# First utterance of an audio tower: the late parts of queries and keys of four heads go from SBUF to SBUF, and ScalarE's queue issues the other eight loads

## The chip, the core and the metric

The kernel runs on one core of one Trainium2 chip. A core has five engines that run their own instruction streams and meet only at semaphores: TensorE (PE, with its weight loads PEld), VectorE (DVE), ScalarE (ACT), GpSimd (POOL) and SyncE (SP), which only issues transfers here. All transfers run on the core's 16 DMA engines. The metric is the device time of one execution in microseconds (us).

## The reference

The input is 16 utterances of 750 frames with 23 features. A time-delay layer (five neighbouring frames, 115 taps, to 128 channels, ReLU, batch normalisation over all frames) gives h. Then come an attention layer and a mixture-of-experts layer, each on the layer norm of h and added to it:

```python
h = relu(patches @ W.T + b); h = batchnorm(h)            # 16 x 746 x 128
q, k, v = heads(layernorm(h) @ Wq.T + bq), ...           # 8 heads of 16
scores = einsum('bhqd,bhkd->bhqk', q, k) / sqrt(16)
h = h + merge(softmax(scores) @ v) @ Wo.T + bo
e = argmax(xf @ Wr + br)                                 # top 1 of 8 experts, xf = layernorm(h)
h = h + gate * (relu(xf @ W1[e] + b1[e]) @ W2[e] + b2[e])   # gate: softmax over one logit, 1
```

## The kernel before, in words

**Stages.** First the time-delay layer of all utterances is computed and kept in `seq`. Then a software pipeline of bodies i = -2 ... 16 follows, each of 72 steps. In body i the scores and probabilities of utterance i are computed, the row maxima of utterance i+1 from step 24 on (and those of utterance i in steps 0 to 23), and layer norm, queries, keys and values of utterance i+2 are prepared. Body -2 (FIRST_BODY) holds only the preparation of utterance 0; body -1 holds the preparation of utterance 1 and, from step 24, the first 48 steps of maxima of utterance 0. At the end tiles of tokens sorted by expert go through their expert's two layers.

**Queries and keys in parts.** A score must be as exact as in float32 but is computed in bf16: each of q and k is split into three bf16 parts (part 0 the rounded value, parts 1 and 2 what is left), made in `q_part` and `k_part` with channels on the 128 partitions. The matmul wants, for each head, 96 partitions: six groups of 16 (n = 0 ... 5), each a part of the head's 16 channels: `Q_PARTS = (0, 0, 1, 1, 0, 2)`, `K_PARTS = (0, 1, 0, 1, 2, 0)`. As heads lie on partitions in `q_part` and beside each other in `q_rows` (in `arena`) and `k_rows`, every part is stored to DRAM (`store_q`, `store_k`: q_parts_dram, k_parts_dram) and loaded from there (`load_parts`, line 506), one transfer for each of the six groups n, for q and for k, for the first four heads (group g = 0) and for the last four (g = 1): 24 loads an utterance. PE's maxima of utterance b start when 12 loads of g = 0 have landed (`pe.wait_ge(s_ld[0], b * 192 + 192)`); those of g = 1 are needed 36 steps later.

**Order of SP in the first two bodies.** Body -2: `store_q` of parts 0, 1, 2, each when its part is there; `store_k(0)`; `load_first_heads`: wait for all three query stores, six query loads, `store_k(1)`, `store_k(2)`, then for each part a wait for that store and its key loads. Body -1 begins with the twelve loads of g = 1. In body -2 `split` runs on DVE (lines 420 to 424), in the others on POOL.

**What else lies there.** At the start of body -1, ACT, DVE and PE compute a few constants (`constants`, lines 1383 to 1390 on PE, 835 to 838 on ACT, 1034 and 1036 on DVE): PE works on a product, ACT copies it out (`wo_t`, line 835), PE goes on with it, and so on, until DVE writes `row_c` (line 1036). POOL waits for that (`s_cv`), then adds to h_cur and writes `seq` (line 710); only then ACT may overwrite `h_cur` with utterance 1 (line 798, two halves at steps 8 and 11, PE's transposes of line 1319 before each). DVE takes its statistics (line 968), POOL merges them, takes the root (line 702) and normalises into xn (line 411, six tiles). At steps 35 and 39 PE transposes xn (line 1319). Each engine works strictly through its own stream, so PE's transpose at step 35 also holds up the maxima that stand behind it; DVE's statistics stand ahead of its first maxima (lines 1192 and 1195: two reductions of 512 columns and one of 468 for three steps). Three PSUM banks lie between PE's score products for the maxima and DVE's reductions.

Of the kernel before, what the change touches and what calls it, by code (L numbers as in the profile page):

```python
# [5 lines left out]
def audio_tower(  # L6
# [33 lines left out]
    L = T - CONTEXT + 1  # L40
    HALF = L // 2
    H = 8
    DH = D // H
# [3 lines left out]
    GH = 4  # L47
# [17 lines left out]

    Q_PARTS = (0, 0, 1, 1, 0, 2)
    K_PARTS = (0, 1, 0, 1, 2, 0)
    KR = len(Q_PARTS) * DH
    KM = KR + 2

# [4 lines left out]
    STEPS = 2 * HALF_STEPS  # L75
# [28 lines left out]
    with ctx:  # L104
# [3 lines left out]
        def sem(name):  # L108
            return ctx.enter_context(nc.semaphore(name))
# [150 lines left out]
        s_q_w = sem("s_q_w")  # L260
        s_k_w = [sem(f"s_k_w{n}") for n in range(3)]
        s_ld = [sem(f"s_ld{g}") for g in range(2)]
        s_mrow = sem("s_mrow")
        s_turn = sem("s_turn")
        s_rt = sem("s_rt")
# [44 lines left out]
        def live(i, ahead):  # L310

            return not isinstance(i, int) or 0 <= i + ahead < B
# [92 lines left out]
        def is_body(i, number):  # L405
            return isinstance(i, int) and i == number
# [56 lines left out]
        def load_patches(engine, c, low, high):  # L463
# [3 lines left out]
            engine.dma_start(patches[CONTEXT * low:CONTEXT * high, t0:t1], taps)\  # L467
                  .then_inc((s_frames if low == 0 else s_rest)[c], 16)

        def load_tok_w(engine, low, high):  # L470
            engine.dma_start(tok_w_sb[CONTEXT * low:CONTEXT * high, :],
                             tok_w.rearrange("(k f) d -> f k d", f=FEAT)[low:high, :, :]).then_inc(s_tokw, 16)
# [6 lines left out]
        def _(sp):  # L479
# [17 lines left out]
            sp.dma_start(rows_dram[DEAD:DEAD + D, :], pad_row[:, :]).then_inc(s_pad, 16)  # L497

            def load_parts(par, g, name, wanted, i, steps):
                dst, src, parts = {"Q": (q_rows, q_dram, Q_PARTS), "K": (k_rows, k_dram, K_PARTS)}[name]  # L500
                for n, part in enumerate(parts):
                    if part in wanted:
                        step = next(steps)
                        if 0 <= i + step // STEPS < B:
                            sp.wait_ge(s_st, scores(i, step))
                        sp.dma_start(dst[par][DH * n:DH * (n + 1), GH * g:GH * (g + 1), 0:L],
                                     src[64 * g:64 * (g + 1), part, :].rearrange("(h j) t -> j h t", j=DH))\
                          .then_inc(s_ld[g], 16)

            def store_q(i, parts):  # L510
                for part in parts:
                    if part == 0:
                        sp.wait_ge(s_free, fill(i, "Q", 1))
                    else:
                        sp.wait_ge(s_split, (i + 2) * 6 + part + 1)
                    sp.dma_start(q_dram[:, part, :], q_part[:, part, :]).then_inc(s_q_w, 16)

            def store_k(i, part):
                if part == 0:
                    sp.wait_ge(s_free, fill(i, "K", 1))  # L520
                else:
                    sp.wait_ge(s_split, (i + 2) * 6 + part + 4)
                sp.dma_start(k_dram[:, part, :], k_part[:, part, :]).then_inc(s_k_w[part], 16)

            def load_first_heads(i, par):
                sp.wait_ge(s_q_w, (i + 2) * 48 + 48)
                steps = iter(LOAD0_AT)
                load_parts(par, 0, "Q", (0, 1, 2), i, steps)
                for part in range(3):
                    if is_body(i, FIRST_BODY) and part > 0:  # L530
                        store_k(i, part)
                for part in range(3):
                    sp.wait_ge(s_k_w[part], (i + 2) * 16 + 16)
                    load_parts(par, 0, "K", (part,), i, steps)

            def body(i, par):
                if live(i, 1):
                    wait(sp, s_st, i * STEPS if live(i, -1) else 0)
                    load_parts(1 - par, 1, "Q", (0, 1, 2), i, iter(LOAD1_AT))
                if live(i, 0):  # L540
                    sp.wait_ge(s_free, fill(i, "MAX1", 0))
                    for n in range(2):
                        sp.dma_start(q_rows[par][KR + n:KR + n + 1, GH:H, :],
                                     max_rows[1][QUAD * n:QUAD * n + GH * NT, :]).then_inc(s_mrow, 16)
                if live(i, 1):
                    load_parts(1 - par, 1, "K", (0, 1, 2), i, iter(LOAD1_AT[6:]))
                if live(i, 2):
                    wait(sp, s_ld[1], (i + 2) * 192)
                    store_q(i, range(3 if is_body(i, FIRST_BODY) else 1))
                    store_k(i, 0)  # L550
                if live(i, 1):
                    sp.wait_ge(s_free, fill(i, "MAX0", 0))
                    for n in range(2):
                        sp.dma_start(q_rows[1 - par][KR + n:KR + n + 1, 0:GH, :],
                                     max_rows[0][QUAD * n:QUAD * n + GH * NT, :]).then_inc(s_mrow, 16)
                if isinstance(i, int) and i == W_LAST + 1:
                    sp.wait_ge(s_ln2, W_LAST + 1)
                    sp.dma_start(w_sb[:, :, W1:W1 + HID], w1.rearrange("e p n -> p e n")).then_inc(s_w, 16)
                    for e in range(E):
                        sp.dma_start(w_sb[:, e, W2:W2 + HID].rearrange("p (j n) -> p j n", j=JH),  # L560
                                     w2[e].rearrange("(j p) n -> p j n", p=128)).then_inc(s_w, 16)
                    sp.dma_start(w_sb[:, :, B2:B2 + D], b2.partition_broadcast(128)).then_inc(s_w, 16)
                    sp.dma_start(w_sb[:, :, B1:B1 + JH], b1).then_inc(s_w, 16)
                if live(i, 2):
                    if not is_body(i, FIRST_BODY):
                        store_q(i, (1, 2))
                        store_k(i, 1)
                        store_k(i, 2)
                    if live(i, 0):
                        sp.wait_ge(s_st, scores(i, HALF_STEPS - 1))  # L570
                    load_first_heads(i, par)
# [199 lines left out]
        def _(act):  # L771
# [35 lines left out]
            def q_or_k(i, name, half, k):  # L807

                full, part, bias, scale = {"Q": (q_full, q_part, bq4, SCALE), "K": (k_full, k_part, bk_sb, 1.0)}[name]
                dst = (full[:, :] if k == 0 else part[:, 0, :])[:, HALF * half:HALF * (half + 1)]  # L810
                if k == 0:
                    act.wait_ge(s_misc, fill(i, name, half))
                    in_turn(act, i, name, half)
                    if name == "Q":
                        wait(act, s_q_w, (i + 2) * 48)
                    else:
                        for n in range(3):
                            wait(act, s_k_w[n], (i + 2) * 16)
                last = nc.scalar.activation(dst, bank(i, name, half)[:, 0:HALF], ACT.Identity, bias=bias[:, 0:1], scale=scale)
                if k == 1:  # L820
                    last.then_inc(s_free, 1)
# [41 lines left out]
            def body(i, par):  # L863
# [4 lines left out]
                for s in range(STEPS):  # L868
# [39 lines left out]
                        nc.scalar.activation(g_exp[:, :], g_diff[:, :], ACT.Exp).then_inc(s_gate, 1)  # L908
                    if s in H_AT and live(i, 3):
                        normed(i + 3, H_AT.index(s))  # L910
                    if is_body(i, LAST_BODY) and s in ACT_SLOTS:
                        n = ACT_SLOTS[s]
                        if n < 0:
                            xt_evac(0, 0)
                        else:
                            act_turn(n, n % ROUND, n // ROUND)
# [371 lines left out]
        def _(pe):  # L1288
# [140 lines left out]
            def body(i, par):  # L1429
# [6 lines left out]
                for s in range(STEPS):  # L1436
# [15 lines left out]
                    if 0 <= b < B:  # L1452

                        u, t, n = m // (3 * NT), m % (3 * NT) // 3, m % 3
                        if m % HALF_STEPS == 0:
                            pe.wait_ge(s_ld[m // HALF_STEPS], b * 192 + 192)
                        wait(pe, s_red, b * STEPS + (m + 1 - N_MX))
                        if n < 2:
                            quad(mx_bank[m % N_MX][:, 0:WIDE_Q], q_rows[b % 2][0:KR, 2 * u + n, D * t:D * (t + 1)],
                                 k_rows[b % 2][0:KR, 2 * u + n, 0:WIDE_Q]).then_inc(s_mx, 1)  # L1460
                        else:
                            for a in range(2):
                                last = quad(mx_bank[m % N_MX][:, NARROW_Q * a:NARROW_Q * (a + 1)],
                                            q_rows[b % 2][0:KR, 2 * u + a, D * t:D * (t + 1)],
                                            k_rows[b % 2][0:KR, 2 * u + a, WIDE_Q:L])
                            last.then_inc(s_mx, 1)
# [65 lines left out]
```

## Time and profile before

| what | us |
|---|---|
| median of 3 runs | 1179.86 (1179.08 to 1182.18) |
| the profiled execution's own time | 1180.77 |
| its span from first to last instruction | 1178.9 |
| PE, DVE, ACT, POOL busy | 1119.5, 1042.9, 912.1, 686.8 |
| first product for maxima of utterance 0 | at 69.28 |

Times in the rows are microseconds from the span's start. PEclk is the granted clock of TensorE: 1.00 is 2.4 GHz and 0.50 is 1.2 GHz. SPq and ACTq are the issuing of transfers by these engines: how long the sequencer was taken up by the issue, not when the data landed. A queue's row such as "x6" is that many issues in a row.

### The profile page before, as it was taken

The page shows a single profiled execution, that of the slowest core. Times are in us where ns is not written, and L with a number is a line of the kernel's source. Part 1 is how long each engine was busy: PE and PEld are TensorE (multiplying, and loading weights), DVE is VectorE, ACT ScalarE, POOL GpSimd, SP SyncE. Part 2 cuts the span into 40 slices and gives each one's busy share as a digit, 9 for nine tenths or more (in the row PEclk, how much of TensorE's full clock was granted, in tenths as well). Part 3 has the DMA queues.
Part 4 walks back from the last instruction along what each step waited for, and adds up shares of the span by engine and source line. Part 5 has one row for each costly group of instructions (what it writes and reads, how often), then busy time and mean ns, then how long its engine had stood idle before and what let it go on. Part 6 is the DMA issues. An engine that isn't in the chain of part 4 may idle for free.

```text
span 1178.9 us, 51282 instructions
## 1 busy us (share of the span) xinstructions
PE 1119.5 (95%) x20483; PEld 728.7 (62%) x20483; DVE 1042.9 (88%) x2404; ACT 912.1 (77%) x2125; POOL 686.8 (58%) x926
## 2 busy tenths in 40 slices
PE   6479999999999999999999999999999999999996
PEld 3323556565656565655656565656565558899996
DVE  8569899999999999999999999999999947777774
ACT  5425888888988888888888888888887885577774
POOL 2052618575766667585858576666653256666664
PEclk9769999999999999999999999999999999999998
DMA  8052121423233231313141323223231623434331
GB/s 199 33 98 83 46 82 43 115 66 96 75 82 94 62 98 52 105 52 107 43 115 61 99 75 84 86 69 97 55 105 38 191 60 92 118 115 117 110 100 47
DMA packets 81192, 102.21 MB, mean 87 GB/s; under 512 B 17964, under 2 KB 74787, under 8 KB 80526
## 3 DMA queue, kind: packets, MB, share of 16 engines
q1 hardware_dynamic: 72416, 79.03, 25.3%
q0 software_dynamic: 8384, 20.22, 5.1%
q8 instruction: 152, 2.49, 0.9%
q14 instruction: 54, 0.44, 0.1%
q10 hardware_dynamic: 186, 0.02, 0.0%
HBM read 60.76 MB, written 38.93 MB: 85 GB/s over the span
## 4 chain that ended last, share of the span: by engine, by line
PE 52%; DVE 36%; DMA 3%; issue 2%; ACT 2%; SPq 1%; DVEq 0%; POOL 0%; POOLq 0%; ACTq 0%
PE psum L1314 27%; DVE half_max L1192 18%; PE psum L1376 9%; DVE half_max L1195 8%; PE psum L1405 7%; PE psum L1417 7%; DVE stats L968 2%; DMA arena<-max_rows 1%; PE psum L1319 1%; DVE by_tok L1008 1%; DVE rows L1049 1%; DVE merged_t L1029 1%; ACT arena L875 1%; PE psum L1396 1%; DVE pos_i L1104 1%
## 5 line engine op out<-in xcount | busy, mean ns | idle before, releaser
L1192 DVE TENSOR_REDUCE half_max<-psum 128x1 f32<-128x512 f32 x768 | 511.4, 677 | 28.9 <-PE psum L1314 28.0
L875 ACT ACTIVATE arena<-psum 128x512 f32<-128x512 f32 (+1 forms) x768 | 423.2, 604 | 61.2 <-PE psum L1314 55.7
L1314 PE MATMUL psum<-k_rows,arena 96*32 96x512 bf16 (+1 forms) x6144 | 462.1, 326 | 8.1 <-DMA k_rows<-k_parts_dram 5.0
L1314 PE MATMUL psum<-arena,k_rows 98*32 98x512 bf16 (+1 forms) x6144 | 457.6, 322 | 4.0 <-DMA arena<-max_rows 2.2
L1376 PE MATMUL psum<-arena,values 128*32 128x234 f32 (+3 forms) x3072 | 313.4, 477 | 1.2 <-ACT arena L878 0.8
L1314 PEld LDWEIGHTS psum<-k_rows,arena 96*32 96x32 bf16 x6144 | 176.8, 97 | 139.8 <-DVE half_max L1192 27.6
L1314 PEld LDWEIGHTS psum<-arena,k_rows 98*32 98x32 bf16 x6144 | 176.9, 96 | 132.1 <-issue 42.1
L1195 DVE TENSOR_REDUCE half_max<-psum 128x2 f32<-128x468 f32 x384 | 242.3, 631 | 2.5 <-PE psum L1314 2.4
L878 ACT ACTIVATE arena<-psum 128x468 f32<-128x468 f32 (+1 forms) x384 | 197.9, 571 | 28.0 <-PE psum L1314 25.4
L665 POOL DMA_INDIRECT routed_rows_dram<-rows,pos_i x96 | 97.0, 1011 | 91.5 <-PE psum L1314 61.5
L646 POOL DMA_INDIRECT out_dram<-k_rest,slot_id x85 | 101.8, 1197 | 61.4 <-DVE k_rest L1170 46.0
L1376 PEld LDWEIGHTS psum<-arena,values 128*32 128x32 f32 (+1 forms) x3072 | 97.9, 110 | 35.2 <-issue 1.8
L676 POOL TENSOR_TENSOR m_diff<-stats 128x6 f32<-128x6 f32 x15 | 3.0, 201 | 141.6 <-DVE stats L968 141.6
L856 ACT COPY xn_t<-psum 128x128 f32<-128x128 f32 x101 | 26.8, 265 | 66.4 <-PE psum L1396 64.8
L1405 PE MATMUL psum<-xn_t,values 128*128 128x128 f32 x536 | 72.2, 278 | 1.3 <-DVE values L1154 1.3
L411 POOL TENSOR_SCALAR arena<-h_cur,m_mean,rstd 128x128 f32<-128x128 f32 x90 | 70.5, 793 | 3.3 <-POOL rstd L702 3.2
L411 POOL TENSOR_SCALAR rows<-rows,n_mean,rstd 128x128 f32<-128x128 f32 x90 | 71.8, 806 | 0.0
L1405 PEld LDWEIGHTS psum<-xn_t,values 128*128 128x128 f32 x536 | 65.9, 194 | 2.6 <-DVE values L1154 1.7
L1154 DVE COPY values<-seq 128x1156 f32 x67 | 53.1, 792 | 9.5
L420 POOL TENSOR_TENSOR q_rest<-q_full,q_part 128x746 f32<-128x746 f32 x15 | 24.2, 1615 | 54.2 <-DVE onehot L1079 37.5
L1008 DVE STREAM_TRANSPOSE by_tok<-o_un 128x384 f32<-128x384 f32 x64 | 36.3, 567 | 12.5 <-ACT o_un L888 12.5
L1405 PE MATMUL psum<-xn_t,seq 128*128 128x128 f32 x272 | 36.7, 278 | 4.2 <-DVE seq L1154 3.7
(237 smaller groups left out, 1603.3 us busy)
## 6 DMA issues: line engine op xcount, KB each, us to landing
arena<-q_parts_dram SPq DMA_DIRECT2D x192, 93.2 KB, 2.6
k_rows<-k_parts_dram SPq DMA_DIRECT2D x192, 93.2 KB, 2.5
q_parts_dram<-q_part SPq DMA_DIRECT2D x48, 186.5 KB
k_parts_dram<-k_part SPq DMA_DIRECT2D x48, 186.5 KB, 1.9
q_full<-routed_rows_dram SPq DMA_DIRECT2D x34, 130.0 KB
k_full<-routed_rows_dram SPq DMA_DIRECT2D x34, 130.0 KB
q_rest<-routed_rows_dram SPq DMA_DIRECT2D x33, 130.0 KB
arena<-in_x_t_dram SPq DMA_DIRECT2D x3, 703.1 KB, 17.0
```

What stands on the lines that cost most here:

```text
L411: last = ops.tensor_scalar(dst(t), src(t), mean_var[:, t, 0:1], r_root[:, t:t + 1], ALU.subtract, ALU.mult)
L646: pool.indirect_dma_start(out=out_rows, out_offset=bass.IndirectOffsetOnAxis(ap=slot_id[:, n:n + 1], axis=0), in_=slot_y[n][:, :], in_offs ...
L665: pool.indirect_dma_start(out=rows_dram, out_offset=bass.IndirectOffsetOnAxis(ap=pos_i[:, t:t + 1], axis=0), in_=rows[:, t, :], in_offset= ...
L875: nc.scalar.activation(probs[0:kn(kt), kt % N_P, j, :], st_bank[s % N_ST][0:kn(kt), 0:WIDE_Q], ACT.Exp).then_inc(s_exp, 1)
L878: nc.scalar.activation(narrow_probs[0:kn(kt), kt, NARROW_Q * j:NARROW_Q * (j + 2)], st_bank[s % N_ST][0:kn(kt), 0:2 * NARROW_Q], ACT.Exp). ...
L1154: nc.vector.tensor_copy(slot_w[n % N_W].unsqueeze(1), w_sb[:, bass.ds(e, 1), :]).then_inc(s_fw, 1)
L1192: nc.vector.tensor_reduce(half_max[:, n, part:part + 1], mx_bank[m % N_MX][:, 0:WIDE_Q], AX.X, ALU.max)\
L1195: nc.vector.tensor_reduce(half_max[:, n, 2:4], mx_bank[m % N_MX][:, 0:2 * NARROW_Q].rearrange("p (a t) -> p a t", a=2), AX.X, ALU.max).the ...
L1314: last = nc.tensor.matmul(dst[n:n + m], weights[:, n:n + m], moving, start=start, stop=stop)
L1376: last = nc.tensor.matmul(o_bank[32 * j:32 * (j + 1), 0:WIDE_Q if wide else NARROW_Q], values[b % 3][0:kn(kt), kt, GH * g + j, :], moving, ...
L1405: last = nc.tensor.matmul(psum[:, 2 + n % 2, D * k:D * (k + 1)], slot_w[n % N_W][:, W1 + D * k:W1 + D * (k + 1)], slot_xt[n % 2][:, :], st ...
L1417: last = nc.tensor.matmul(psum[:, 5 + n % 2, 0:D], slot_ht[n % 2][:, D * k:D * (k + 1)], slot_w[n % N_W][:, W2 + D * k:W2 + D * (k + 1)], ...
```

## The change

In body -2 SP stores part 0 and 1 of q and part 0 of k as before. For g = 0 the groups that hold part 2 of q (one), part 1 of k (two) and part 2 of k (one) no longer come from DRAM: SP copies them from `q_part` and `k_part` straight into `q_rows` and `k_rows`, one transfer for each group and head, 16 in all, each of 16 partitions. After them SP stores the three late parts (they are still loaded from DRAM for g = 1) and waits for all stores. The other eight loads of g = 0 are issued by ACT at the end of body -2, ahead of its share in `constants`: five for q after two q stores have landed, three for k after the store of part 0. PE waits for both groups of transfers. In every other body SP does what it did; ACT and PE get one wait more, in body -1, on a semaphore of the copies.

```diff
+    DIRECT = (("Q", 2), ("K", 1), ("K", 2))
+    N_DIRECT = Q_PARTS.count(2) + K_PARTS.count(1) + K_PARTS.count(2)
...
+        def load_rows(engine, par, g, name, n):
+            dst, src, parts = {"Q": (q_rows, q_dram, Q_PARTS), "K": (k_rows, k_dram, K_PARTS)}[name]
+            engine.dma_start(dst[par][DH * n:DH * (n + 1), GH * g:GH * (g + 1), 0:L],
+                             src[64 * g:64 * (g + 1), parts[n], :].rearrange("(h j) t -> j h t", j=DH))\
+                  .then_inc(s_ld[g], 16)
...
+            def direct(i, par, name, part):
+
+                dst, src, parts, k = {"Q": (q_rows, q_part, Q_PARTS, 1), "K": (k_rows, k_part, K_PARTS, 4)}[name]
+                sp.wait_ge(s_split, (i + 2) * 6 + part + k)
+                for n in range(len(parts)):
+                    if parts[n] == part:
+                        for h in range(GH):
+                            sp.dma_start(dst[par][DH * n:DH * (n + 1), h, 0:L], src[DH * h:DH * (h + 1), part, :])\
+                              .then_inc(s_direct, 16)
+
+            def first_heads(i, par):
+
+                store_q(i, (0, 1))
+                store_k(i, 0)
+                for name, part in DIRECT:
+                    direct(i, par, name, part)
+                sp.wait_ge(s_q_w, 32)
+                store_q(i, (2,))
+                store_k(i, 1)
+                store_k(i, 2)
+                sp.wait_ge(s_q_w, 48)
+                for part in range(3):
+                    sp.wait_ge(s_k_w[part], 16)
...
             def body(i, par):
+                if is_body(i, FIRST_BODY):
+                    first_heads(i, par)
+                    return
...
                     if name == "Q":
                         wait(act, s_q_w, (i + 2) * 48)
+                        if is_body(i, FIRST_BODY + 1):
+                            act.wait_ge(s_direct, GH * N_DIRECT * 16)
...
+                    if is_body(i, FIRST_BODY) and s == STEPS - 1:
+                        act.wait_ge(s_q_w, 32)
+                        for n in (0, 1, 4, 2, 3):
+                            load_rows(act, par, 0, "Q", n)
+                        act.wait_ge(s_k_w[0], 16)
+                        for n in (0, 2, 5):
+                            load_rows(act, par, 0, "K", n)
...
                         if m % HALF_STEPS == 0:
-                            pe.wait_ge(s_ld[m // HALF_STEPS], b * 192 + 192)
+                            if b == 0 and m == 0:
+                                pe.wait_ge(s_direct, GH * N_DIRECT * 16)
+                            pe.wait_ge(s_ld[m // HALF_STEPS], b * 192 + 192 - (0 if m else 16 * N_DIRECT))
```

## Rows read from the trace of the kernel before

**Rows 1.** The page's chain that ended last, by engine

```profile
PE 52%; DVE 36%; DMA 3%; issue 2%; ACT 2%; SPq 1%; DVEq 0%; POOL 0%; POOLq 0%; ACTq 0%
```

**Rows 2.** The chain, 30 to 110 us: start, us, what

```profile
55.76 2.52 DMA q_parts_dram<-q_part
...
65.60 3.64 DMA k_rows<-k_parts_dram
...
69.28 3.15 PE psum L1314 x30
...
79.55 2.38 PE psum L1314 x25
```

**Rows 3.** Timeline of SP's queue: start, us, line, transfer, issues

```profile
53.12 2.96 SPq L516 DMA_DIRECT2D q_parts_dram<-q_part  x3
56.13 0.43 SPq L523 DMA_DIRECT2D k_parts_dram<-k_part  x1
58.30 2.68 SPq L506 DMA_DIRECT2D arena<-q_parts_dram  x6
...
66.06 2.77 SPq L506 DMA_DIRECT2D arena<-q_parts_dram  x6
```

**Rows 4.** Waits, 40 to 75 us: total, times, longest

```profile
PE psum L1314 <- DMA k_rows<-k_parts_dram: 5.0, 1, 5.0
```

**Rows 5.** Timeline of ACT, 56 to 77 us; idle before in brackets

```profile
56.51 0.48 ACT L829 COPY values<-psum 128x384 f32<-128x384 f32 x1
57.64 0.27 ACT L835 COPY o_un<-psum 128x128 f32<-128x128 f32 x1 [0.65 <-PE psum L1384]
...
62.82 0.48 ACT L798 COPY h_cur<-psum 128x384 f32<-128x384 f32 x1 [2.98 <-POOL seq L710]
64.35 0.48 ACT L798 COPY h_cur<-psum 128x384 f32<-128x384 f32 x1 [1.05 <-PE psum L1319]
```

**Rows 6.** Timeline of PE in the same stretch

```profile
58.60 0.57 PE L1387 MATMUL psum<-wv_sb,o_un 128*128 128x8 f32 x2 [0.99 <-DVE bo_all L1034]
...
63.36 0.90 PE L1319 MATMUL psum<-ident,h_t 128*128 128x128 f32 x3 [2.13 <-ACT h_cur L798]
...
75.85 0.90 PE L1319 MATMUL psum<-ident,arena 128*128 128x128 f32 x3
```

**Rows 7.** Timeline of DVE, 53 to 70 us

```profile
57.32 0.94 DVE L424 TENSOR_TENSOR k_part<-k_rest,k_part 128x746 bf16<-128x746 f32 x1
...
64.86 1.26 DVE L968 BATCH_NORM_STATS2 stats<-h_cur 128x6 f32<-128x128 f32 x6 [4.17 <-ACT h_cur L798]
...
69.95 1.29 DVE L1192 TENSOR_REDUCE half_max<-psum 128x1 f32<-128x512 f32 x2 [3.83 <-PE psum L1314]
```

**Rows 8.** Timeline of POOL, 60 to 76 us

```profile
60.99 1.80 POOL L710 TENSOR_TENSOR seq<-h_cur,bo_all 128x768 f32<-128x768 f32 x1
66.20 0.20 POOL L676 TENSOR_TENSOR m_diff<-stats 128x6 f32<-128x6 f32 x1 [3.41 <-DVE stats L968]
...
69.65 4.69 POOL L411 TENSOR_SCALAR arena<-h_cur,m_mean,rstd 128x128 f32<-128x128 f32 x6 [0.22 <-POOL rstd L702]
```

**Rows 9.** ACT's own queue at the kernel's start, its only issues

```profile
0.80 0.40 ACTq L773 DMA_DIRECT2D tok_b_sb<-in_tok_b_dram  x1
1.23 1.39 ACTq L471 DMA_DIRECT2D by_tok<-in_tok_w_dram  x1
```

**Rows 10.** Stretches: PE, PEld, DVE, ACT, POOL busy, PEclk, DMA share, GB/s

```profile
58.00:60.00 2.00, 0.98 (x4) 0.72 (x4) 0.45 (x2) 0.33 (x2) 0.00 (x0) 0.50 0.31 70
...
66.00:68.00 2.00, 0.00 (x0) 0.00 (x0) 0.12 (x1) 0.01 (x1) 1.49 (x8) 0.50 1.05 154
...
80.00:82.00 2.00, 2.00 (x40) 1.10 (x36) 1.28 (x3) 0.30 (x2) 0.00 (x0) 0.62 0.00 0
...
94.00:96.00 2.00, 1.40 (x22) 0.59 (x26) 2.00 (x6) 0.51 (x2) 1.92 (x2) 0.79 0.00 0
```

**Rows 11.** Small transfers issued by SP at the start (0.1 KB)

```profile
30.80 0.61 SPq L493 DMA_DIRECT2D bv_sb<-in_bv_dram  x1
```

More of the change, by code:

```diff
@@ L262, in audio_tower @@
         s_ld = [sem(f"s_ld{g}") for g in range(2)]
+        s_direct = sem("s_direct")
         s_mrow = sem("s_mrow")
@@ L499, in load_parts @@
             def load_parts(par, g, name, wanted, i, steps):
-                dst, src, parts = {"Q": (q_rows, q_dram, Q_PARTS), "K": (k_rows, k_dram, K_PARTS)}[name]
-                for n, part in enumerate(parts):
+                for n, part in enumerate({"Q": Q_PARTS, "K": K_PARTS}[name]):
                     if part in wanted:
@@ L505, in load_parts @@
                             sp.wait_ge(s_st, scores(i, step))
-                        sp.dma_start(dst[par][DH * n:DH * (n + 1), GH * g:GH * (g + 1), 0:L],
-                                     src[64 * g:64 * (g + 1), part, :].rearrange("(h j) t -> j h t", j=DH))\
-                          .then_inc(s_ld[g], 16)
+                        load_rows(sp, par, g, name, n)
+            def direct(i, par, name, part):
[18 more added lines that the diff above has]
+                    sp.wait_ge(s_k_w[part], 16)
             def store_q(i, parts):
@@ L529, in load_first_heads @@
                 for part in range(3):
-                    if is_body(i, FIRST_BODY) and part > 0:
-                        store_k(i, part)
-                for part in range(3):
                     sp.wait_ge(s_k_w[part], (i + 2) * 16 + 16)
@@ L548, in body @@
                     wait(sp, s_ld[1], (i + 2) * 192)
-                    store_q(i, range(3 if is_body(i, FIRST_BODY) else 1))
+                    store_q(i, (0,))
                     store_k(i, 0)
@@ L564, in body @@
                 if live(i, 2):
[L565 to L568, printed above, removed]
+                    store_q(i, (1, 2))
+                    store_k(i, 1)
+                    store_k(i, 2)
                     if live(i, 0):
```

## The prediction

> **What bounds the kernel now.** I read the page's chain first: nine tenths of it are PE and DVE [rows 1], so transfers matter only where both stand still. The chain of the stretch in question, ahead of the first maxima, is different: store of q part 2 (2.52 us), loads and key stores behind it, the last key load (3.64), and then PE at 69.28 [rows 2]. The waits say what that costs: PE idles 5.0 us before its first product for maxima, on a key load [rows 4]. PE had finished its last earlier work at 63.36 + 0.90 = 64.26 [rows 6]. So the loads are late by 5.0 us, and that is what the change can attack.
>
> Next I read what stands behind. PE transposes xn at 75.85, in its place among the maxima (step 35) [rows 6]. POOL finishes xn at 69.65 + 4.69 = 74.34 [rows 8]. So if the maxima started earlier, PE would get to step 35 earlier, but xn would be there only at 74.34: of the 5.0 us only 75.85 - 74.34 = 1.5 us can be won as long as POOL's chain stays where it is. The bound after the change is therefore not the loads but the chain that makes xn. Back from POOL's 69.65: merge from 66.20 [rows 8], DVE's statistics from 64.86 [rows 7], ACT's two copies into h_cur at 62.82 and 64.35, the first waiting for POOL's line 710 [rows 5], which starts at 60.99 [rows 8] after DVE's last constant, and that chain of constants passes through ACT's copy of wo_t at 57.64 [rows 5]. Nothing in it has slack: from 58.60 on each row starts as the one before ends.
>
> **The change part by part.**
>
> *ACT's eight issues.* They stand in ACT's stream between the values copy, which ends at 56.51 + 0.48 = 56.99, and the copy of wo_t at 57.64 [rows 5]. First ACT waits for two q stores. The third store went out at 55.76 and took 2.52 us [rows 2]; the second goes out one DVE subtraction (0.94, [rows 7] shows its twin) earlier, at 54.8, so it lands near 57.3. An issue costs SP (2.68 + 0.04) / 6 = 0.45 us, and (2.77 + 0.05) / 6 = 0.47 when the DMA engines are full [rows 3]. ACT's own two issues took 0.40 and 1.39 us [rows 9]: these are the two ends. I take 0.46, since the transfers are those that SP issued, unchanged in shape, and ACT's first issue (0.40) is near to it. The k store of part 0, now issued ahead of the third q store's place, at 56.13 at the latest [rows 3], lands before the sixth load's turn. ACT is done at 57.3 + 8 x 0.46 = 61.0.
>
> *What waits behind them.* The copy of wo_t starts at 61.0 instead of 57.64, 3.4 late. PE's line 1387 had waited until 58.60 for DVE as well [rows 6]; now it starts 0.05 after wo_t's 0.27, at 61.3: 2.7 us late. All that follows is a chain without slack and moves by 2.7: POOL's line 710 to 63.7, ACT's h_cur copies to 65.5 and 67.1, PE's second transpose of h_t to 66.1, done at 67.0, DVE's statistics to 67.6, done at 68.85, POOL's normalisation to 72.35, done at 77.05.
>
> *The loads.* Eight by ACT from 57.3 on (746 KB), sixteen copies by SP (16 x 23.9 KB = 382 KB): the same bytes as twelve loads before. The DMA engines were used to 0.31 from 58 to 60 and to 1.05 from 66 to 68, where they moved 154 GB/s [rows 10]; at that pace 1.13 MB need 7.3 us, and part of it starts at 55.8: landed by about 64.5 to 65.5. ACT's last load is issued at 60.5 and takes at most the 3.64 of the last key load [rows 2]: 64.2.
>
> *SP's sixteen copies.* Four follow the q split (about 55.8), eight and four the k splits, whose last ends at 58.26 [rows 7]. The issues bound them, not the splits: 55.8 + 16 x 0.46 = 63.2, and the last one, issued at 62.8, lands between 2.52 and 3.64 later [rows 2]: 65.3 to 66.4. No row shows a copy from SBUF to SBUF. Ends for an issue: 0.40, the smallest that ACT's queue shows [rows 9], and 0.61 with 0.04 between two, the small ones of SP at the start [rows 11]; the latter puts the last issue at 65.6 and its landing at 69.2. The far end is the 1.39 [rows 9], rival D. I take 0.46, as a store and loads of unlike shape cost SP nearly the same, 0.43 and 0.45 [rows 3]. The three late stores then go out at about 63.3 to 64.7 and land near 68, so the twelve loads of the other four heads begin at about 68 instead of 66.06 and end at 73.6; they are needed 36 steps after the first product, near 88. That is hidden, and would cost something only beyond 14 us.
>
> *First maxima.* PE is free at 67.0, the data are there at 66.4. So PE starts at about 67.0 instead of 69.28. DVE's statistics, which stand ahead of its first reduction, end at 68.85, so DVE starts at 68.9 instead of 69.95: 1.05 us of lead. At DVE's pace, the same as before, PE would be at step 35 at 75.85 - 1.05 = 74.8. There xn is missing until 77.05. PE starts that transpose at 77.1 instead of 75.85, idle 2.3 us and DVE with it, and everything behind it is 77.1 - 75.85 = 1.25 us late. The 5.0 us wait on loads is thus gone, and a wait on POOL stands in its place.
>
> *From there to the end.* From 75.9 to the end the chain is PE and DVE with small parts of others, so I let 1.25 us go through undiminished. The additional waits on landed copies are passed long before. The sum: 1180.77 + 1.25 = 1182.0 against the profiled execution. Against the median of the runs, which is 0.9 lower, it is 1181.1, and this is my number.
>
> *The clock.* The granted clock is 0.50 from 58 on and rises near 81 (0.62 in 80 to 82), when the query products begin, and is 0.79 in 94 to 96 [rows 10]. Until 81.94 the chain is on PE [rows 2], so a rise that comes later or earlier relative to the work counts. The wait of 2.3 us lies in a stretch that is at 1.2 GHz anyway. I put nothing for it and keep 1 us to each side.
>
> *Rules of the Trainium skill.* The trace shows full DMA engines (1.05) only from 60 on [rows 10] and SP issuing one load every 0.46 us. "DMA: Bandwidth & Descriptors", section "Issuing engines are not separate DMA queues", says that issuing from several engines saves only the sequencer's time for the issue, as all run on the same 16 DMA engines. By that rule the transfers gain only what lay in SP's sequence; it agrees with the bound by bytes above. The same page, "Rules for kernel authors", says that transfers under 64 KB pay mostly overhead; it speaks against sixteen copies of 23.9 KB, and by it they would be the last to land, as they are in my working too; their landing at 69.2 by the dearer issue would still leave the sum as it is.
>
> **The rivals.**
>
> *A, forecast: ACT's issues push the constants.* 1181.1, as worked out. For it: the stream order and the absence of slack.
>
> *B: ACT's issuing is cheap or does not hold up its copies.* Then POOL's chain stays, xn is there at 74.34, the maxima start with the data at about 66, PE waits at step 35 until 74.35: 1.5 us won, 1178.4. Against it: ACT's queue shows 0.40 and 1.39, nothing near zero [rows 9].
>
> *C, the other side: ACT's issues are dear.* If an issue on ACT's queue beside a busy SP costs the 1.39 [rows 9], eight cost 11.1 us, ACT is free at 68.4, wo_t's successor is 10.1 late, xn at 84.4, and the loss is 84.45 - 75.85 = 8.6: 1188.5. It becomes slower by more than 3.5 us from about 0.74 us for an issue on. Against it: the 1.39 is one transfer of another shape, at a time when the whole input was being loaded.
>
> *D: the copies come late.* Before, step 35 came 75.85 - 69.28 = 6.57 after the first product. Landed at 69.2 they bring it at 75.8, still before xn's 77.05, and the result is A's. They decide only if they land after 77.05 - 6.57 = 70.5, that is from 0.74 us an issue on; at 0.9 they are there at 55.8 + 15 x 0.9 + 3.64 = 72.9, step 35 comes at 79.5, 3.7 late: 1183.6. Nothing but the 1.39 speaks for it.
>
> **How the numbers follow.** About 0.3%, 3.5 us, is what a measurement can tell from no change. A 0.66, B 0.15, C 0.12, D 0.07. A and B lie within 0.3% wholly, up to noise of runs (the three shown span 3.1 us); of C three quarters are over it, of D half; noise and the clock put a little on both sides. Slower 0.14, same 0.82, faster 0.04. The range takes in B's 1178.4 and D's 1183.6 with something for noise: 1178.2 to 1184.3; what is left out is mostly C.
>
> **What would show it.** In the profile after: eight ACTq issues of 0.43 to 0.47 us between 57 and 61; the copy of wo_t at about 61; PE's first product for maxima near 67 and DVE's first reduction near 68.9; PE's wait at step 35 on POOL's line 411, about 2.3 us, ending near 77.1; scores of utterance 0 starting at 100.4 instead of 99.2. A is wrong if wo_t is copied before 60 (B), after 63 (C), if the first product waits on a transfer until after 70 (D), or if the time leaves 1178 to 1184.

## The result and the profile after

| | before | after |
|---|---|---|
| median of 12 runs, us | 1180.13 (1177.32 to 1182.18) | 1182.86 (1180.96 to 1185.69) |
| ratio, 95% interval | | 1.0023 [1.0014, 1.0032] |
| the profiled execution and its span, us | 1180.77, 1178.9 | 1184.05, 1182.0 |
| first product for maxima | 69.28 | 67.81 |
| PE's transpose of xn, step 35 | 75.85 | 78.14 |

The change costs 2.7 us, 0.23%: real by its interval, and less than the 0.3% that I had set as the bound of a change. It is also more than the 1.25 that I had forecast: 1.25 us are a ratio of 1.0011, just below the interval. Of the eleven executions of e1_sp_issues below, one took 4211.93 us and is left out of its ratio. The first maxima do start 1.5 us earlier; the time is lost behind them. The wait on loads [rows 4] is gone and another has taken its place. Waits of the kernel after, 40 to 78 us (total, times, longest):

```profile
PE psum L1352 <- DVE half_max L1230: 1.1, 1, 1.1
...
PEld psum L1352 <- DMA k_rows<-k_part: 0.3, 1, 0.3
```

and, in the same view up to 85 us, the one that counts:

```profile
PE psum L1357 <- POOL arena L414: 2.5, 1, 2.5
```

The timeline of ACT after shows where it comes from. In [rows 5] the copy of wo_t (L835 there, L866 here; the profile calls the tile o_un, whose memory wo_t uses) began 0.65 us behind the end of the values copy; now eight issues stand between:

```profile
56.81 0.48 ACT L860 COPY values<-psum 128x384 f32<-128x384 f32 x1
57.03 2.90 ACTq L475 DMA_DIRECT2D arena<-q_parts_dram  x5
59.97 1.86 ACTq L475 DMA_DIRECT2D k_rows<-k_parts_dram  x3
61.87 0.27 ACT L866 COPY o_un<-psum 128x128 f32<-128x128 f32 x1 [4.57 <-issue]
...
66.44 0.48 ACT L827 COPY h_cur<-psum 128x384 f32<-128x384 f32 x1 [2.99 <-POOL seq L739]
```

SP's queue after. The sixteen copies (L523) take 0.62 to 0.63 us each (2.48 / 4, 7.54 / 12), and the late stores follow only then:

```profile
56.08 2.48 SPq L523 DMA_DIRECT2D arena<-q_part  x4
58.60 7.54 SPq L523 DMA_DIRECT2D k_rows<-k_part  x12
66.25 0.50 SPq L546 DMA_DIRECT2D q_parts_dram<-q_part  x1
66.80 0.91 SPq L553 DMA_DIRECT2D k_parts_dram<-k_part  x2
71.59 2.67 SPq L475 DMA_DIRECT2D arena<-q_parts_dram  x6
```

PE, DVE and POOL after, to be laid beside [rows 6 to 8]. PE's products start, stop for DVE's statistics, go on, and then PE stands before step 35 until POOL's row is over (73.28 + 4.72 = 78.00; xn lies in `arena`, so the rows call it that):

```profile
66.98 0.90 PE L1357 MATMUL psum<-ident,h_t 128*128 128x128 f32 x3 [2.13 <-ACT h_cur L827]
67.81 1.44 PE L1352 MATMUL psum<-k_rows,arena 96*32 96x512 bf16 x16
70.39 5.23 PE L1352 MATMUL psum<-k_rows,arena 96*32 96x512 bf16 x48 [1.14 <-DVE half_max L1230]
78.14 0.87 PE L1357 MATMUL psum<-ident,arena 128*128 128x128 f32 x3 [2.53 <-POOL arena L414]
```

```profile
68.48 1.26 DVE L1006 BATCH_NORM_STATS2 stats<-h_cur 128x6 f32<-128x128 f32 x6 [4.17 <-ACT h_cur L827]
69.66 1.27 DVE L1230 TENSOR_REDUCE half_max<-psum 128x1 f32<-128x512 f32 x2
```

```profile
64.61 1.80 POOL L739 TENSOR_TENSOR seq<-h_cur,bo_all 128x768 f32<-128x768 f32 x1
...
73.28 4.72 POOL L414 TENSOR_SCALAR arena<-h_cur,m_mean,rstd 128x128 f32<-128x128 f32 x6 [0.21 <-POOL rstd L731]
```

The chain of the kernel after has no transfer in this stretch any more; it goes through POOL:

```profile
73.28 0.81 POOL arena L414
...
74.10 3.91 POOL arena L414 x5
78.01 0.14 issue
78.14 0.87 PE psum L1357 x3
```

The delay lasts. In the chains of the two kernels the long row of score products of utterance 0 begins at 99.19 before and at 101.41 after, 2.22 later, where step 35 was 2.29 later:

```profile
99.19 5.63 PE psum L1314 x92
```

```profile
101.41 5.63 PE psum L1352 x92
```

### The profile page after: what moved, and what is told of

The parts are those of the page before. It is cut to its first block, busy times and chain, and to the rows that moved or that the text cites. A ratio compares the mean times of both kernels' runs of the same rounds, so it can differ in the third digit from the quotient of the medians.

```text
span 1182.0 us, 51298 instructions
## 1 busy us (share of the span) xinstructions
PE 1121.0 (95%) x20483; PEld 730.0 (62%) x20483; DVE 1043.7 (88%) x2404; ACT 913.0 (77%) x2125; POOL 690.0 (58%) x926
## 4 chain that ended last, share of the span: by engine, by line
PE 50%; DVE 37%; issue 3%; DMA 2%; ACT 2%; POOL 1%; SPq 0%; DVEq 0%; POOLq 0%; ACTq 0%
PE psum L1352 25%; DVE half_max L1230 19%; PE psum L1414 9%; DVE half_max L1233 8%; PE psum L1443 7%; PE psum L1455 6%; DVE stats L1006 2%; DMA arena<-max_rows 1%; PE psum L1357 1%; DVE by_tok L1046 1%; DVE rows L1087 1%; DVE merged_t L1067 1%; ACT arena L906 1%; PE psum L1434 1%; DVE pos_i L1142 1%
```

## The experiments

The end of the values copy, from which everything here is counted, lies at 56.99 in the profile of before and at 55.9 to 58.3 in the others: executions differ by that much before they come to the changed part: the second store of q stands as much earlier or later in each. So the table gives distances from that end, one profiled execution each, and the time from all runs. "Start" is the first product for maxima, "step 35" PE's transpose of xn, "against before" the difference of step 35 to the first row. "At the scores" is the same difference for ACT's first exponential of utterance 0, some 24 us behind step 35.

| kernel | wo_t | xn ready | start | step 35 | against before | at the scores | ratio to before |
|---|---|---|---|---|---|---|---|
| before | 0.65 | 17.35 | 12.29 | 18.86 | | | 1 |
| after | 4.58 | 20.71 | 10.52 | 20.85 | +1.99 | +1.92 | 1.0023 [1.0014, 1.0032] |
| e1_sp_issues | 0.65 | 17.38 | 14.01 | 20.58 | +1.72 | +2.92 | 1.0012 [1.0000, 1.0024] |
| e4_before_idle | 3.25 | 19.34 | 13.32 | 19.89 | +1.03 | +1.09 | 1.0004 [0.9994, 1.0015] |
| e5_no_copies | 3.65 | 19.77 | 9.88 | 19.92 | +1.06 | +1.21 | 1.0013 [1.0004, 1.0022] |
| e3_gaps | 0.65 | 16.78 | 10.16 | 16.92 | -1.94 | -1.82 | 0.9988 [0.9977, 1.0000] |
| e3_gaps_again | 0.64 | 17.23 | 10.18 | 17.37 | -1.49 | -0.32 | 0.9990 [0.9978, 1.0002] |
| e7_gaps_no_copies | 0.65 | 17.37 | 10.17 | 17.51 | -1.35 | -0.53 | 0.9978 [0.9967, 0.9989] |
| e2_after_constants | 0.64 | 18.04 | 11.72 | 18.29 | -0.57 | +0.62 | 0.9990 [0.9977, 1.0003] |
| e6_after_idle | 9.63 | 25.75 | 15.58 | 25.89 | +7.03 | +7.09 | 1.0059 [1.0041, 1.0077] |

In every row step 35 comes at the later of two: 0.14 or 0.15 behind xn, or 6.57 behind the start. The start decides in the kernel before, in e1_sp_issues, in e4_before_idle and in e2_after_constants, xn in the others. The theory is that the time follows the column of step 35; the rivals were the copies, the transfers' traffic and the start itself. Times 1180 us, each ratio's interval holds its row's difference at step 35 (for the change 1.7 to 3.8, for e7_gaps_no_copies -3.9 to -1.3).

The column of the scores is less tidy. In e1_sp_issues, e2_after_constants, e3_gaps_again and e7_gaps_no_copies 0.8 to 1.2 us are lost between step 35 and the scores. In these four executions the granted clock rises later: PEclk is 0.62 in 80 to 82 before [rows 10] and 1.00 in 82 to 84, and in the last three it is 0.50 and then 0.81 to 0.89, though step 35 stands 1.0 to 1.6 us earlier in the span than before; in e1_sp_issues it is 0.50 until 86, with step 35 only 2.7 us later. e7_gaps_no_copies, columns as in [rows 10]:

```profile
80.00:82.00 2.00, 2.00 (x32) 0.76 (x28) 1.18 (x3) 1.03 (x2) 0.00 (x0) 0.50 0.04 8
```

No experiment moves the clock alone, so it is likely but not shown that the late rise costs this microsecond, and nothing shows how many other executions have it. The intervals of e1_sp_issues, e2_after_constants and e7_gaps_no_copies leave out what their one profiled execution has at the scores: one profile stands for the order of events, and only the runs for the time.

**e1_sp_issues: ACT issues nothing.** The edit, on the kernel after:

```diff
-                for name, part in DIRECT:
-                    direct(i, par, name, part)
+                direct(i, par, "Q", 2)
+                sp.wait_ge(s_q_w, 32)
+                for n in (0, 1, 4, 2, 3):
+                    load_rows(sp, par, 0, "Q", n)
+                sp.wait_ge(s_k_w[0], 16)
+                for n in (0, 2, 5):
+                    load_rows(sp, par, 0, "K", n)
+                direct(i, par, "K", 1)
+                direct(i, par, "K", 2)
...
-                    if is_body(i, FIRST_BODY) and s == STEPS - 1:
-                        act.wait_ge(s_q_w, 32)
-                        for n in (0, 1, 4, 2, 3):
-                            load_rows(act, par, 0, "Q", n)
...
```

> The change with the eight loads issued by SP itself, between the copies of q part 2 and those of k; ACT issues nothing. Theory (ACT's eight issues hold up its copy of wo_t and with it xn): wo_t is copied near 57.7 again, POOL starts line 739 near 61.0 and ends xn near 74.4; SP issues 24 transfers from 55.8 on, which at 0.46 us each end at 66.8 and land near 69.5, so the first product comes at 69.5 and step 35 at 76.0: time as before, 1180.1 (ratio to before 1.000). If a copy from SBUF costs SP 0.62 us by its kind, as in the profile of the change, and not because ACT issues beside it, the sixteen copies show 0.62 here too, SP ends at 69.5, the first product comes at 72 and the time is 2.5 us above before. Rival (the copies themselves or the order of stores cost the 2.7 us): 2.7 above before with wo_t early.

Its SP queue and PE timeline:

```profile
56.70 2.47 SPq L523 DMA_DIRECT2D arena<-q_part  x4
59.22 2.45 SPq L475 DMA_DIRECT2D arena<-q_parts_dram  x5
61.72 1.36 SPq L475 DMA_DIRECT2D k_rows<-k_parts_dram  x3
63.12 7.47 SPq L523 DMA_DIRECT2D k_rows<-k_part  x12
```

```profile
71.94 6.64 PE L1352 MATMUL psum<-k_rows,arena 96*32 96x512 bf16 x64 [6.74 <-DMA k_rows<-k_part]
```

xn is back at its old distance (17.38), and the start is 1.7 late, because a copy from SBUF costs SP 0.62 us with no other queue at work, where a load in the same queue costs 0.49 or 0.45 (2.45 / 5, 1.36 / 3). So 0.62 is the price of this kind of copy: the second reading of the expectation, though 2.5 us was too much for it. With ACT silent the copies leave the chain of xn as it was; what they cost is the late start. The time (1.0000 to 1.0024) separates this run clearly neither from before nor from the change, so here the profile speaks and not the time.

**e4_before_idle: eight useless issues on ACT in the kernel before.** Nothing waits for them but ACT itself, in the last body.

```diff
...
+                    if is_body(i, FIRST_BODY) and s == STEPS - 1:
+                        for n in range(8):
+                            act.dma_start(idle_in[:, n, :, :], x_t[0:16, 0:4, 8 * n:8 * (n + 1)]).then_inc(s_idle, 16)
...
```

> The kernel before with eight more transfers, issued by ACT at the end of body -2, that nobody needs: 16 partitions by 4 pieces of 32 bytes each, 2 KB, so the engines carry nothing to speak of. All loads stay with SP. Theory: the eight issues alone push wo_t to 60.7 (0.46 each, if the 0.60 seen in the change came from two queues issuing at once) or 61.8 (0.60 each, if it is ACT's own price); xn ends 2.7 to 3.7 later than 74.34; the maxima still start at 69.3 with the loads; PE transposes xn at 77.1 to 78.1 instead of 75.85; time 1.2 to 2.3 above before, 1181.4 to 1182.4. Rival (the late xn is harmless, the loss of the change came from its transfers): time as before, 1180.1.

```profile
56.37 0.35 ACTq L916 DMA_DIRECT2D idle_in<-in_x_t_dram  x1
...
56.75 3.34 ACTq L916 DMA_DIRECT2D idle_in<-in_x_t_dram  x7
60.13 0.27 ACT L837 COPY o_un<-psum 128x128 f32<-128x128 f32 x1 [3.24 <-issue]
```

```profile
58.06 2.67 SPq L508 DMA_DIRECT2D arena<-q_parts_dram  x6
```

ACT pays 0.48 an issue (3.34 / 7) and xn is 2.0 later, not the 2.7 or more of the expectation. The useless issues wait for no store, so they began at 56.37, half a microsecond before the values copy ended, and wo_t is only 2.60 late (3.25 - 0.65). Of that PE had waited 0.64 for DVE anyway: its next product began at 58.60 [rows 6], and could have begun 0.05 behind wo_t's end, at 57.64 + 0.27 + 0.05 = 57.96. Then 1.4 of slack at step 35 (18.86 - 17.35 - 0.14) swallow most of the 2.0, and what moves step 35 by 1.0 is the start, itself 1.0 late: SP's six key loads took 4.55 instead of 4.06, and from their end to the start 3.93 passed instead of 3.26. Why is open. The time cannot be told from before. This run shows that ACT's issues delay xn, and that alone, with the slack still there, it costs next to nothing; it does not show what a late xn costs. It shows one thing more: ACT's last four issues run beside SP's six loads without a pause (58.06 to 60.73), and neither queue is slower for it: 0.48 on ACT, and 2.67 for SP's six where they took 2.68 before [rows 3].

**e5_no_copies: ACT issues as in the change, the late groups come from DRAM.**

```diff
...
-                for name, part in DIRECT:
-                    direct(i, par, name, part)
                 sp.wait_ge(s_q_w, 32)
                 store_q(i, (2,))
                 store_k(i, 1)
                 store_k(i, 2)
                 sp.wait_ge(s_q_w, 48)
-                for part in range(3):
-                    sp.wait_ge(s_k_w[part], 16)
+                load_rows(sp, par, 0, "Q", 5)
+                sp.wait_ge(s_k_w[1], 16)
+                load_rows(sp, par, 0, "K", 1)
+                load_rows(sp, par, 0, "K", 3)
+                sp.wait_ge(s_k_w[2], 16)
+                load_rows(sp, par, 0, "K", 4)
+                sp.wait_ge(s_k_w[0], 16)
...
```

> The change without the copies on chip: ACT issues the same eight loads at the same place, SP stores all three parts of q and k and then loads the four late groups from DRAM, as before the change. Theory: the ACT chain is as in the change, so wo_t at 60.8 to 61.9, xn at 77.1 to 78.0, time as the change, 1.2 to 2.5 above before. It tells what an ACT issue costs when SP issues hardly anything beside it (five stores and loads in place of sixteen copies): 0.46 if the price came from two queues at once, 0.60 if it is ACT's own. First product near 67. Rival (the copies cost the time): as before, 1180.1.

Its ACT queue and PE timeline:

```profile
56.94 2.30 ACTq L472 DMA_DIRECT2D arena<-q_parts_dram  x5
59.28 1.50 ACTq L472 DMA_DIRECT2D k_rows<-k_parts_dram  x3
60.83 0.27 ACT L854 COPY o_un<-psum 128x128 f32<-128x128 f32 x1 [3.64 <-DMA q_parts_dram<-q_part]
```

```profile
67.06 1.44 PE L1340 MATMUL psum<-k_rows,arena 96*32 96x512 bf16 x16 [0.23 <-DMA k_rows<-k_parts_dram]
...
77.10 0.87 PE L1345 MATMUL psum<-ident,arena 128*128 128x128 f32 x3 [2.53 <-POOL arena L411]
```

The same shapes issued at the same place cost ACT 0.46 to 0.50 here and 0.58 to 0.62 in the change: without SP's sixteen copies beside them they have the price that I had predicted, and step 35 is 1.06 late, near my 1.25. The loads from DRAM are there at 9.88. That is no proof that they are faster than the copies: in the change PE was busy until it started at 10.52, and the trace has the last copy landed at 67.44, distance 10.15. Where PE waits for nothing but the transfers, the two are level, 10.16 with copies (e3_gaps) and 10.17 without (e7_gaps_no_copies). The copies are not needed for the early start, and with them ACT's issues are dearer. That is read from the profiles: the intervals of the times, 1.0004 to 1.0022 here and 1.0014 to 1.0032 in the change, overlap.

**e3_gaps: the eight issues in ACT's idle time.** One ahead of the copy of wo_t, two behind it, five behind the last constant; the copies stay.

```diff
...
                 nc.scalar.copy(wo_t, st_bank[0][:, 0:D]).then_inc(s_ca, 1)
+                for n in (1, 4):
+                    load_rows(act, 0, 0, "Q", n)
...
                 if is_body(i, FIRST_BODY + 1):
                     constants()
+                    for n in (2, 3):
+                        load_rows(act, 1 - par, 0, "Q", n)
+                    act.wait_ge(s_k_w[0], 16)
+                    for n in (0, 2, 5):
+                        load_rows(act, 1 - par, 0, "K", n)
...
                         act.wait_ge(s_q_w, 32)
-                        for n in (0, 1, 4, 2, 3):
-                            load_rows(act, par, 0, "Q", n)
-                        act.wait_ge(s_k_w[0], 16)
-                        for n in (0, 2, 5):
-                            load_rows(act, par, 0, "K", n)
+                        load_rows(act, par, 0, "Q", 0)
```

> The change with ACT's eight issues spread over the idle time in its share of the constants: one ahead of the copy of wo_t (0.65 us idle there), two behind it (1.6 us idle), five after the last constant (3.0 us idle); copies by SP as in the change. Theory: no copy of ACT is delayed by more than 0.3 us, POOL starts line 739 near 61.0, xn ends near 74.4; the loads are issued by 62.9 and land near 66, SP's copies near 67.5, the first product comes near 67.5 and step 35 near 74.4: 1.5 us below before, 1178.7, and 4.2 below the change. Rival (transfers or the clock hold up the start whoever issues): first product near 69, time as before or above.

```profile
58.09 0.36 PE L1428 MATMUL psum<-wv_sb,o_un 128*128 128x8 f32 x2 [0.94 <-DVE bo_all L1075]
...
66.70 6.64 PE L1355 MATMUL psum<-k_rows,arena 96*32 96x512 bf16 x64 [3.51 <-DMA k_rows<-k_part]
73.46 0.87 PE L1360 MATMUL psum<-ident,arena 128*128 128x128 f32 x3
```

The same transfers from the same queues as in the change, only elsewhere in ACT's stream: step 35 is 3.9 us earlier than in the change, and the time 0.9988 and, once more as e3_gaps_again, 0.9990, where step 35 is 3.5 earlier. Neither interval alone excludes before; both exclude the change's 1.0023. Half a microsecond of this profile is not the edit's: PE's constant took 0.36 here and 0.57 in [rows 6], at a PEclk of 0.82 in 58 to 60 instead of 0.50 [rows 10], and xn came 0.57 earlier than before. e3_gaps_again has xn within 0.12 of before.

> The kernel of e3_gaps once more, to narrow its interval beside e7_gaps_no_copies: 1.4 to 2 us below before, ratio 0.9983 to 0.9988.

**e7_gaps_no_copies: e3_gaps with the edit of e5_no_copies.**

> ACT's eight issues spread over its idle time as in e3_gaps, but no copies on chip: SP stores the late parts and loads the four late groups from DRAM as in e5_no_copies. In e5_no_copies the last of those loads let PE start at 67.06, about as early as the copies did in e3_gaps (66.70, with the values copy there 0.6 earlier). Theory (the gain of e3_gaps is that the eight loads leave SP's queue without holding up ACT, and xn then bounds; the copies do nothing for it): PE transposes xn within 0.3 us of where it does in e3_gaps, counted from the end of the values copy (16.9 us behind it; 18.9 in the kernel before), time 1.4 below before, 1178.6. Rival (the copies are what makes the early start possible): first product as in the kernel before, time 1180.

Its ACT, PE and POOL timelines:

```profile
56.87 0.48 ACT L848 COPY values<-psum 128x384 f32<-128x384 f32 x1
57.19 0.35 ACTq L472 DMA_DIRECT2D arena<-q_parts_dram  x1
58.00 0.27 ACT L854 COPY o_un<-psum 128x128 f32<-128x128 f32 x1 [0.65 <-PE psum L1413]
58.01 0.83 ACTq L472 DMA_DIRECT2D arena<-q_parts_dram  x2
...
60.76 1.39 ACTq L472 DMA_DIRECT2D k_rows<-k_parts_dram  x3
63.19 0.48 ACT L817 COPY h_cur<-psum 128x384 f32<-128x384 f32 x1 [2.98 <-POOL seq L729]
```

```profile
67.52 6.64 PE L1343 MATMUL psum<-k_rows,arena 96*32 96x512 bf16 x64 [2.89 <-DMA k_rows<-k_parts_dram]
74.86 0.88 PE L1348 MATMUL psum<-ident,arena 128*128 128x128 f32 x3 [0.70 <-POOL arena L411]
```

```profile
70.02 4.70 POOL L411 TENSOR_SCALAR arena<-h_cur,m_mean,rstd 128x128 f32<-128x128 f32 x6 [0.22 <-POOL rstd L721]
```

Step 35 follows xn by 0.14, with half of the change left out. Its distance of 17.51 is within the expected 0.3 of e3_gaps_again's 17.37, not of e3_gaps's 16.92, which had the faster constants. The time is 1178.07, ratio 0.9978 [0.9967, 0.9989]: it beats the kernel before by 2.3 us by the medians, more than the 1.4 that was expected, and the change by about 5 us (0.9978 against 1.0023). Whether it is better than e3_gaps the intervals do not tell.

**e2_after_constants: all eight issues behind the last constant.**

```diff
                 if is_body(i, FIRST_BODY + 1):
                     constants()
+                    act.wait_ge(s_q_w, 32)
+                    for n in (0, 1, 4, 2, 3):
+                        load_rows(act, 1 - par, 0, "Q", n)
+                    act.wait_ge(s_k_w[0], 16)
+                    for n in (0, 2, 5):
+                        load_rows(act, 1 - par, 0, "K", n)
...
```

> The change with all eight of ACT's issues in one place behind its last constant, where it is idle for 3.0 us before it copies h_cur. Theory: 8 x 0.60 = 4.8 us there (SP issues copies beside it) delay the h_cur copy by 1.8 us, or by 0.7 at 0.46 each; xn ends 0.7 to 1.8 later than in the kernel before, less the 1.5 of slack at step 35: between 0.8 below and 0.3 above before, 1179.3 to 1180.4, which is 2.3 to 3.4 below the change. Rival (any issue on ACT costs the same wherever it stands): as the change, 1182.9.

```profile
58.10 0.34 ACTq L475 DMA_DIRECT2D arena<-q_parts_dram  x1
...
58.47 1.98 ACTq L475 DMA_DIRECT2D arena<-q_parts_dram  x4
60.49 1.85 ACTq L475 DMA_DIRECT2D k_rows<-k_parts_dram  x3
62.45 0.48 ACT L827 COPY h_cur<-psum 128x384 f32<-128x384 f32 x1 [4.02 <-issue]
```

The h_cur copy waits for the end of the issues, about 1.1 us, and xn is 0.7 late; step 35 comes 0.57 earlier than before. It is not xn that sets it here but the start, at 11.72 (11.72 + 6.57 = 18.29): the copies, issued as early as in e3_gaps, landed 1.5 us later than there. The expectation had not seen that, and why they did is open. By the profile it is a dearer place than the gaps and a cheaper one than ahead of the constants; the times exclude the change (the interval ends at 1.0003) but do not tell this place from the gaps. The price of an issue depends on what it stands in front of.

**e6_after_idle: the eight useless issues, in the change, behind its own eight.**

> The change with eight more transfers of 2 KB on ACT, behind its eight loads and ahead of its copy of wo_t, that nobody needs (64 pieces of 32 bytes each). Theory (each issue on ACT ahead of the constants is paid in full once xn is the bound): 8 x 0.46 to 0.60 = 3.7 to 4.8 us on top of the change, PE's transpose of xn that much later, first product 3.7 to 4.8 later too, as PE's transposes of h_t wait in the same chain: 1186.5 to 1187.6. Rival (something behind hides it, or the loss of the change came from elsewhere): 1183.

```profile
62.89 5.03 ACTq L953 DMA_DIRECT2D idle_in<-in_x_t_dram  x8
67.96 0.27 ACT L868 COPY o_un<-psum 128x128 f32<-128x128 f32 x1 [9.63 <-issue]
```

Eight issues of 2 KB each cost 5.03 us, move xn by 25.75 - 20.71 = 5.04 and the time from 1.0023 to 1.0059, 4.2 us (six runs; the two intervals together allow about 2 to 6.5); the profiled step 35 is 7.03 behind that of before and the time 0.0059 x 1180 = 7.0. Against e4_before_idle, where nearly the same issues cost nothing that the time shows, this is the whole point: the slack at step 35, about 1.4 us, is spent once, and from then on every issue is paid in full, at 0.63 here beside SP's copies and 0.48 there.

## Why the prediction was right, point by point

- **The bound.** Right, and nearly in size: the 1.5 us that the loads' 5.0 could give are 1.4, as PE starts the transpose 0.14 behind xn. e3_gaps_again and e7_gaps_no_copies got 1.5 and 1.35 at step 35, e3_gaps 1.9 with an xn that was 0.57 early by itself, the change nothing.
- **ACT's issues hold up the constants, and no slack follows.** Right, and shown: wo_t is 3.93 late by the table, POOL's line 739 3.32 and xn 3.36, which is 3.93 less the 0.64 that PE had waited for DVE anyway, as the prediction had subtracted (3.4 to 2.7). Taking the issues out of the way (e3_gaps, e7_gaps_no_copies) gives it back; doubling them (e6_after_idle) adds their full duration.
- **The price of an issue on ACT.** The mis-sized term: 0.46 taken, 2.94 / 5 = 0.59 and 0.62 measured with the gaps between, so 4.8 us for eight instead of 3.7: 1.1 us. e5_no_copies shows that 0.46 to 0.50 is right without the copies beside.
- **The copies.** 0.62 instead of 0.46, near the upper row that I had cited [rows 11] (and 23.3 KB each by the profile, not 23.9). The last one was issued at 65.5 and landed at 67.44, before D's 70.5, so D did not come; the twelve loads of the other heads began at 71.59, 3.6 later than I said, as SP's late stores were issued only from 66.25 on and took until then to land, and nothing waited for them.
- **The start.** 67.81 against 67.0, DVE's first reduction at 69.66 against 68.9: the 0.8 that the dearer issues add. PE waited 2.53 on POOL, 2.3 predicted.
- **The sum.** 1.25 predicted, 2.29 in the profile, 1.04 more: 1.1 from the dearer issues, less 0.27 because they began at 57.03 and not at 57.3, and 0.2 in small pieces on the way (PE's start 0.14 behind xn instead of 0.05, and rows a little longer). By the distances of the table, which take out that the first stage ended 0.30 later in this execution, it is 1.99. At the scores it is 2.22 in the span, 101.41 where I had said 100.4. The medians differ by 2.7 [1.7, 3.8 by the interval]. That the rest, 0.4 to 0.7, is anything but the spread of runs is not shown. The mechanism was right and the number only fair: the measured loss is twice the forecast one, and it lies in my range in part because that was drawn wide enough for D, which did not come.
- **The clock.** PEclk is 0.62 in 80 to 82 before [rows 10]; after, it is 0.50 there and 0.58 in 82 to 84. Worked out from these means, the rise came at about 81.5 and 83.7, 2.2 later, as step 35 did: for this pair the zero in the sum held. In four of the other executions the rise did not move with the work, so the zero is partly luck.
- **Rivals.** B, issues that do not hold up copies, is refuted by every run with all eight issues ahead of wo_t: its copy comes at 3.25 to 9.63 instead of 0.65. C, dear issues, was to cost 3.5 us from 0.74 an issue on; the change, at 0.60, lies between the forecast and C.

## What to carry to other kernels

Before a wait is attacked, find the second bound behind it: here 5.0 us of waiting were worth 1.5. In this kernel a transfer's issue took its engine about half a microsecond in the stream (0.46 to 0.63 back to back), for 2 KB as for 93 KB; handed to an idle queue it is free only in that engine's idle time, so look at what stands behind it in the order, and spread the issues over the gaps. Splitting a transfer into four multiplies the issues, and they may come to be the bound in place of the bytes: the sixteen copies held SP's queue for 10.0 us, and brought no earlier start than four loads. And look behind the step where you measure: a lead of 1.4 us there was down to 0.3 to 0.5 by the scores in two executions whose clock rose late.

## What the runs showed of the hardware

- A copy between SBUF tensors of 16 partitions by 1492 bytes took SP's queue 0.62 us an issue, in the change (7.54 / 12), and with ACT's queue silent (7.47 / 12); a load of four times the bytes from DRAM 0.45 to 0.49 (2.68 / 6 before, 2.45 / 5 in e1_sp_issues).
- ACT's queue took 0.46 to 0.50 us an issue with no copies beside it (e5_no_copies, e4_before_idle) and 0.58 to 0.63 beside SP's copies (the change, e6_after_idle), for loads of 93 KB and of 2 KB alike. The copies do not always do this: in e2_after_constants ACT's first five loads took 0.48 each beside them (58.10 to 60.49) and only the last three 0.62 (1.85 / 3). What decides is not shown.
- It is not the second queue as such. SP's loads from DRAM beside ACT's issues slowed neither (e4_before_idle: 0.48 on ACT, 2.67 for SP's six where they took 2.68 alone), and SP's copies took 0.63 beside ACT's issues and 0.62 without them.
